# Content lambdas image by image in quarters of TensorE's columns, with their sums and scaling

## What is computed

```python
b, d, n1, n2 = x.shape
n = n1 * n2
xf = x.reshape(b, n, d)
softmax_keys = jax.nn.softmax(xf @ Wk.T, axis=1)
values = _bn(xf @ Wv.T, gamma_v, beta_v, axes=(0, 2), ch_shape=(1, -1, 1))
queries = (xf @ Wq.T).reshape(b, n, k_dim, h).transpose(0, 2, 1, 3)
queries = _bn(queries, gamma_q, beta_q, axes=(0, 2, 3), ch_shape=(1, -1, 1, 1))
content_lambda = jnp.einsum('bmk,bmv->bkv', softmax_keys, values)
position_lambdas = jnp.einsum('nmk,bmv->bnkv', E, values)
content_output = jnp.einsum('bknh,bkv->bhvn', queries, content_lambda)
position_output = jnp.einsum('bknh,bnkv->bhvn', queries, position_lambdas)
return (content_output + position_output).reshape(b, d, n1, n2)
```

## Time and profile before

| | |
|---|---|
| median of three runs | 1447.19 us (1446.07 to 1447.33) |
| the profiled execution, its own time | 1447.59 us |
| its span in the trace | 1445.6 us |
| PE busy | 1430.4 us, 99% of the span |
| DVE, ACT, POOL busy | 852.0, 757.0, 424.6 us |
| granted PE clock, mean | 0.999 |
| DMA | 134.68 MB, 93 GB/s over the span |

### The profile page before, as it was taken

The page is one execution under the profiler, slowest core; times in us unless marked ns, Lnnn a source line. Parts: engine busy times, 40 slices in busy tenths (PEclk is TensorE's granted clock), DMA queues, the critical chain, the costliest instruction groups (busy, mean ns, idle before and its releaser), DMA issues.

```text
span 1445.6 us, 36192 instructions
## 1 busy us (share of the span) xinstructions
PE 1430.4 (99%) x14608; PEld 1191.8 (82%) x14608; DVE 852.0 (59%) x1226; ACT 757.0 (52%) x1109; POOL 424.6 (29%) x366
## 2 busy tenths in 40 slices
PE   8999999999999999999999999999999999999998
PEld 7997888888888888888888888888888888888886
DVE  7989565555555555555555555555555555555553
ACT  6775555555455555554555455544555455545552
POOL 6683233223322332133212331233223322332130
PEclk9999999999999999999999999999999999999999
DMA  8845322434152422434152333424252333425221
GB/s 308 289 156 93 84 66 66 87 94 94 40 120 65 110 63 75 93 93 89 44 123 65 95 65 87 94 75 85 65 123 65 72 80 94 94 53 107 65 58 30
DMA packets 342684, 134.68 MB, mean 93 GB/s; under 512 B 206864, under 2 KB 338048, under 8 KB 342144
## 3 DMA queue, kind: packets, MB, share of 16 engines
q1 hardware_dynamic: 342656, 134.31, 38.6%
HBM read 109.12 MB, written 25.17 MB: 93 GB/s over the span
## 4 chain that ended last, share of the span: by engine, by line
PE 97%; DVE 1%; DMA 0%; issue 0%; ACT 0%; SPq 0%; POOL 0%; POOLq 0%; DVEq 0%
PE ps_a L1224 81%; PE ps_b L1241 5%; PE ps_a L1208 4%; PE ps_b L1104 3%; PE ps_a L1094 1%; PE ps_b L1163 1%; DMA x_main<-in_x 0%; DVE bn L719 0%; DVE q_stats L744 0%; DVE v_stats L738 0%; DVE key_diag L782 0%; POOL v_rstd L459 0%; PE ps_b L1179 0%; DVE top_level L774 0%; DVE top_level L773 0%
## 5 line engine op out<-in xcount | busy, mean ns | idle before, releaser
L1224 PE MATMUL ps_a<-v_hi,e_hi 128*128 128x512 f32 x1708 | 670.8, 393 | 0.0
L1224 PE MATMUL ps_a<-v_hi,e_lo 128*128 128x512 f32 x1708 | 664.7, 389 | 0.0
L657 ACT ACTIVATE q_diag<-q_blk,q_shift_n,q_scale_n 128x256 f32<-128x256 f32 x512 | 411.2, 868 | 42.9 <-PE ps_b L1241 42.9
L575 ACT ACTIVATE e_hi<-e_nat 128x512 fp32r<-128x512 f32 x305 | 192.8, 633 | 442.2 <-PE ps_a L1224 435.6
L1224 PE MATMUL ps_a<-b_lo,e_hi 128*128 128x512 f32 x976 | 379.6, 389 | 0.0
L1224 PEld LDWEIGHTS ps_a<-v_hi,e_hi 128*128 128x128 f32 x1708 | 320.5, 188 | 67.3
L1224 PEld LDWEIGHTS ps_a<-v_hi,e_lo 128*128 128x128 f32 x1708 | 320.7, 188 | 64.7
L486 POOL TENSOR_TENSOR e_nat<-e_nat,s_buf 128x512 f32<-128x512 f32 x61 | 79.7, 1306 | 920.2 <-DVE e_lo L749 920.2
L854 DVE TENSOR_TENSOR pos<-ps_a,content 128x512 f32<-128x512 f32 x183 | 126.6, 692 | 296.0 <-PE ps_a L1224 296.0
L749 DVE TENSOR_TENSOR e_lo<-e_nat,e_hi 128x512 fp32r<-128x512 f32 x305 | 290.7, 954 | 1.7 <-ACT e_hi L575 1.4
L1224 PE MATMUL ps_a<-t_lo,e_hi 128*128 128x512 f32 x732 | 285.4, 390 | 0.0
(11 more groups left out here) (133 smaller groups left out, 890.3 us busy)
## 6 DMA issues: line engine op xcount, KB each, us to landing
e_nat<-in_L_conv_E SPq DMA_DIRECT2D x128, 512.0 KB, 4.8
res<-in_x SPq DMA_DIRECT2D x64, 256.0 KB, 5.9
out_dram<-res SPq DMA_DIRECT2D x60, 256.0 KB, 4.7
x_main<-in_x SPq DMA_DIRECT2D x24, 512.0 KB, 6.0
q_dram<-q_nat SPq DMA_DIRECT2D x4, 2048.0 KB, 7.6
q_blk<-q_dram SPq DMA_DIRECT2D x32, 256.0 KB, 2.9
x_more<-in_x SPq DMA_DIRECT2D x8, 512.0 KB, 8.6
out_dram<-res SPq DMA_DIRECT2D x4, 192.0 KB, 3.7
```

The source lines that it names most:

```text
L575: nc.scalar.activation(e_hi[:, i], e_source(i, slot), ACT.Copy).then_inc(e_hi_ready, 1)
L657: ins = nc.scalar.activation(to[:, n], of, ACT.Identity, bias=q_shift_n[:, n:n + 1], scale=q_scale_n[:, n:n + 1])
L1224: ins = nc.tensor.matmul(BANK_OF[i], e[:, i, j].rearrange("p n k -> p (n k)"), v[:, j], start=(STARTS[i] and j == 0 and n == 0), stop=(STO ...
```

## The change

The content lambdas are now computed for each image alone: 16 key columns with 32 value columns, image (g, a) on quarter a of PE's columns. All results lie in one bank, as `lam_ps`, 256 columns wide: row 32a + k, column 32g + v. The sums are taken in the same way, 32 matmuls of 16 x 1 in place of four of 128 x 1. `lam_scale` has no masks: for each quarter a reciprocal of 16 x 8 and a product of 16 x 256 that writes only the wanted blocks of `lam_diag` (the rest was zeroed at the start). `inv_mask` is gone; `inv_sum` has 8 columns. Nothing else in the program changes; lines behind L909 have numbers lower by up to three.

```diff
-        inv_sum = sb("inv_sum", [P, B // TN])
-        inv_mask = sb("inv_mask", [P, B // TN, A])
+        inv_sum = sb("inv_sum", [P, G])
...
-        sum_ps, q_ps = ps_b[:, 0, P:P + B // TN], ps_b[:, 0, 0:2]
+        sum_ps, q_ps = ps_b[:, 0, P:P + G], ps_b[:, 0, 0:2]
         gn_ps = ps_b[:, 1, 0:GB * 12]
+        lam_ps = ps_b[:, 0, BANK:BANK + G * V]
...
                 dve.wait_ge(lam_summed, 1)
-                link(nc.vector.reciprocal(inv_sum[:], sum_ps))
-                masks = row_mask[:].rearrange("p (h a) -> p h a", a=A)
-                for half in range(2):
-                    rows = slice(half * HALF, (half + 1) * HALF)
-                    ins = nc.vector.tensor_tensor(inv_mask[rows], inv_sum[rows].unsqueeze(2).to_broadcast([HALF, B // TN, A]),
-                                                  masks[rows, half].unsqueeze(1).to_broadcast([HALF, B // TN, A]), ALU.mult)
+                for a in range(A):
+                    rows = slice(a * V, a * V + KD)
+                    ins = nc.vector.reciprocal(inv_sum[rows], sum_ps[rows])
                 link(ins)
                 dve.wait_ge(lam_zeroed, 1)
-                for half in range(2):
-                    rows = slice(half * HALF, (half + 1) * HALF)
-                    nc.vector.tensor_tensor(
-                        lam_diag[rows].rearrange("p (s h a v) -> p h s a v", h=2, a=A, v=V)[:, half],
-                        ps_b[rows].rearrange("p i (s f) -> p (i s) f", s=2)[:, :, 0:P].rearrange("p s (a v) -> p s a v", v=V),
-                        inv_mask[rows].unsqueeze(3).to_broadcast([HALF, B // TN, A, V]), ALU.mult).then_inc(lam_masked, G // 2)
+                for a in range(A):
+                    rows = slice(a * V, a * V + KD)
+                    nc.vector.tensor_tensor(lam_diag[rows].rearrange("p (g a v) -> p a g v", a=A, v=V)[:, a],
+                                            lam_ps[rows].rearrange("p (g v) -> p g v", v=V),
+                                            inv_sum[rows].unsqueeze(2).to_broadcast([KD, G, V]), ALU.mult
+                                            ).then_inc(lam_masked, G // A)
...
-                    for s in range(B // TN):
-                        for h in range(2):
-                            g = 2 * s + h
-                            ins = nc.tensor.matmul(ps_b[h * HALF:(h + 1) * HALF, s // 2, (s % 2) * BANK:(s % 2) * BANK + P],
-                                                   keys[:, j, g].rearrange("p a k -> p (a k)"), v_nat[:, j, g * P:(g + 1) * P],
-                                                   start=(j == 0), stop=(j == J - 1))
+                    for g in range(G):
+                        for a in range(A):
+                            ins = nc.tensor.matmul(lam_ps[a * V:a * V + KD, g * V:(g + 1) * V], keys[:, j, g, a],
+                                                   v_nat[:, j, (g * A + a) * V:(g * A + a + 1) * V],
+                                                   start=(j == 0 and g == 0), stop=(j == J - 1), skip_group_check=True)
                 ins.then_inc(lam_half, 1)
...
                 pe.wait_ge(exp_summed, A)
-                for s in range(B // TN):
-                    ins = nc.tensor.matmul(sum_ps[:, s:s + 1], exp_sum[:, s * P:(s + 1) * P], ones[:], start=True, stop=True)
+                for g in range(G):
+                    for a in range(A):
+                        ins = nc.tensor.matmul(sum_ps[a * V:a * V + KD, g:g + 1],
+                                               exp_sum[:, (g * A + a) * KD:(g * A + a + 1) * KD], ones[:], start=True, stop=True)
                 ins.then_inc(lam_summed, 1)
```

## The result

| | before | after |
|---|---|---|
| median | 1447.19 us (1446.07 to 1447.33) | 1454.71 us (1453.54 to 1454.97, 5 runs) |
| the profiled execution, its own time | 1447.59 us | 1453.54 us |
| its span in the trace | 1445.6 us | 1451.6 us |
| PE, DVE busy | 1430.4, 852.0 us | 1430.0, 853.6 us |

The change makes the kernel slower: ratio 1.0052, 95% interval 1.0041 to 1.0063, some 7.5 us. The forecast was 1447.7 us, with a range of 1446.5 to 1449.8; it is wrong.

A forecast was written before the change was run, and what follows sets the result against it. PE bounds the kernel, through the start of L1179; its 2.35 us gain becomes waiting for DVE, 0.52 us later. 1447.59 + 0.52 gives 1448.1; the median lies 0.4 below the profiled execution: 1447.7 us, range 1446.5 to 1449.8.

The forecast's parts named there:

- The half of the lambdas: Content lambdas on PE (L1163): a half of 256 rows takes 2.30 us, 1.34 us less than before.
- a half over 4 us: Sign in the new profile, at the lambdas on PE, that the forecast is wrong.
- DVE sets the start of `lam_scale`: Ahead of the content spread (L1179): `lam_scale` still starts at 133.58 us, behind DVE's unchanged queue, not tied to PE.
- DVE's part: `lam_scale` on DVE: four reciprocals and four products take 2.58 us, 0.52 more than before; bounds -0.1 to +1.3.
- The key sums: Key sums on PE (L1171): 64 rows at the query's price take 0.69 us, 0.10 us gained.
- rival 4: Key sums keep 99 ns a row, 6.3 us in all; L1179 starts 3.2 us late, 1450.4 us; chance 0.03.
- Rival 3: Column quarters on PE run in turn, 31 ns a row; L1179 starts 9.7 us late, 1456.9 us; chance 0.03.
- The rule of a start every 25 ns: Skill's rule for PE matmuls: 576 rows would take 14.4 us, estimate 1453.5 us; the query's rows speak against it.
- Rival 1: PE's clock falls in the 2.9 us gap before L1179, costing 1.4 us: 1449.1, up to 1450.6 us; chance 0.21.
- Rival 5: SBUF tensors 64 bytes lower, L1224's operands among them: a quarter per cent of pace is 2.9 us either way; chance 0.04.
- The residual's loads start 2.35 us earlier: Loads that wait for the key sums start 2.35 us earlier; nothing on the chain waits for them.

The follow-up runs named there:

- bursts of 128 rows: Changed kernel with its lambda matmuls in four bursts of 64, eight wide matmuls between two bursts, instead of two bursts of 256 rows; 1449.78 us, ratio 1.0018.
- the second padded: Changed kernel with four bursts of 64 lambda matmuls and 64 unused bytes that restore the SBUF addresses; 1449.2 us, ratio 1.0012.
- two images: Changed kernel with 32 key by 64 value columns per matmul, 128 rows in a half, parity masks, addresses as before the change; 1448.83 us, ratio 1.0009.
- E before the residual: Changed kernel with E for pair 2 loaded ahead of the residual, whose second load waits for its first; 1453.02 us, ratio 1.0037.
- the padded one: Changed kernel with 64 unused bytes where `inv_mask` was, so later SBUF tensors stand as before the change; 1453.35 us, ratio 1.0039.
- 128 more: Changed kernel with 32 one-column matmuls (128 PE instructions) added behind the warming transposes; 1453.01 us, ratio 1.0046.
- the rows longer: Changed kernel with the same number of lambda matmuls, each with 128 moving value columns instead of 32; one run, 1457.75 us.
- the narrow matmuls on the kernel before: Kernel before the change with its 30 warming transposes replaced by 256 narrow matmuls (512 rows) on the identity; one run, 1456.19 us.

## Why the prediction was wrong

**The half of the lambdas: the step that failed.** "A half is then 0.15 + 256 x 0.0084 = 2.30 us." The pace was nearly right: 191 rows in 1.78 us, 9 ns a row, and a half without its stall takes 2.44 us. The length was not: the price came from queries of 128 rows and was stretched to 256, with the supply of PE's instructions put at nothing. The halves took 4.92 and 4.40 us by the chain, 2.6 and 2.1 more than forecast, of which 2.48 and 1.96 are the stalls, in which PE waits for a fetch of its instructions. The rows that gave the price could not have shown it, since a query lies between long products. The profile of the kernel before had one row on supply, the instruction queue with its 18 packets, and the prediction did not use it; so the bound from above should have been wide. The signal that was named for this, a half over 4 us, came in.

**DVE sets the start of `lam_scale`.** "Nothing in the trace ties the start of `lam_scale` to PE" was true of a PE that is early. With stalls and slow clock PE's sums come at 135.6, two microseconds behind the end of L761, and DVE waits 1.84 us. Where the stalls are short or gone the forecast's order holds: the spread at 136.24 and 136.42 with bursts of 128 rows (the second padded), forecast 136.30, with PE waiting 0.5 and 1.6 us for DVE; and at 135.94 with two images, with 2.7 us.

**DVE's part: right.** 2.58 us were forecast; 0.85 + 0.10 + 1.78 = 2.7 were measured, from 135.67 to 138.40. Neither group of four overlaps: the four products of 420 ns each take 1.78 us.

**The key sums: right.** 0.67 us, 0.69 forecast; rival 4, with 99 ns a row, is out. Rival 3 (quarters in turn) is out too. The rule of a start every 25 ns (the Trainium skill, TensorE: Matmul & The Clock Gate, "Wait — 56ns, not 53.3ns?") fails for such narrow matmuls on column quarters: 9 ns between starts here. Its estimate of 1453.5 lay near the result, by a mechanism that no trace shows.

**Rival 1, the clock: it came, in another place.** Not in a gap ahead of the spread but behind the two stalls, at some 129.9 us, for 1.62 us (1.4 asked). That the stalls caused it is read from order alone: the three experiments that keep both stalls whole (E before the residual, the padded one, 128 more) have a block of 5.44 to 5.47 us as well, and where the bursts are shorter or the rows longer the clock stays at 1.00 there. In the narrow matmuls on the kernel before it is at 0.50 from 109 us, within the second stall. After one wait of 2.7 us it once held and once fell.

**Rival 5, the addresses: it came, in another part.** Priced as a pace of the loop's matmuls, which did not change. It acts on loads, and counts through the next point.

**"The residual's loads start 2.35 us earlier; nothing on the chain waits for them."** They started 3.7 us later (135.66 instead of 131.95), took SP 10.10 us to issue instead of 8.02 (8.10 with the padding), and the load of E behind them feeds ACT's queue, in which q_diag of the first query stands. This chain was costed at nothing as a step that moves forward; that it would be on the path when it moves back was not asked. It cost 1.3 us up to the query.

**The tail** had no step at all: 0.9 us, and the median's last 1.5 us are not explained.

The chances failed in the same way. The rivals stood beside one another, each with the rest of the kernel as forecast; the result is mostly one missing mechanism, the supply of instructions, that set off the clock and the late loads and moved the last fetch into the last stores.

## What to carry to other kernels

Before a product is cut into many narrow ones, count PE's instructions in the longest stretch with nothing long between them: here 128 rows in a burst (256 instructions with weight loads) nearly held, 256 rows stood still for two microseconds at a block's border, and moving the bursts apart gave back 4.7 of 7.5 us. Where PE waits on "issue", look for the packets of the instruction queue: their times told what the chain of waits could not. A price per row from short bursts holds for short bursts only. And where the engine that is made faster is not the one that sets the end of the stage, ask what its being late would release: the queue of loads behind its semaphore had 1.3 us in it.

## What was not expected of the hardware

- PE's supply: blocks of 256 instructions, one in 4.8 us when PE waited for each of them, with DMA busy beside it; stalls of 2.0 to 2.5 us at a border in the changed kernel, with the DMA quiet. Each stall ends 1.2 to 1.6 us after a packet of the instruction queue.
- Narrow fp32 matmuls on quarters of the columns start every 9 ns.
- 64 bytes in the place of a load's target in SBUF: `res` 5.9 or 6.6 us, `q_blk` 2.9 or 3.3.
- A store of the output takes 1.3 to 2.0 us to issue instead of 0.49 when PE's last packet of instructions starts around it, and the end of the kernel comes 0.9 to 1.5 us later.
